# A two-layer graph network on one NeuronCore: the first edge pass takes its scores in one tile of 32 nodes by 512 edges

## The reference, cut to what matters

```python
h  = node_features @ node_fc_W + node_fc_b
hs, hd = h[src], h[dst]
a = jnp.sum(hs * hd, axis=-1)                      # one score per edge
g = sigmoid(... edge features ...)                 # three relation logits per edge
alpha = _seg_softmax(a, dst, n)                    # softmax over the edges of one destination
beta  = _seg_softmax(g, dst, n)
s_att = jnp.einsum('ed,kdf->ef', hs, node_att_W)
h_att = segment_sum(alpha[:, None] * s_att, dst) / kk
t_rel = jnp.einsum('ed,mdf->emf', hs, rel_att_W)
h_rel = segment_sum(jnp.einsum('em,emf->ef', beta, t_rel), dst) / mm
h_red = relu(concatenate([h_att, h_rel]) @ out_fc_W + out_fc_b)
```

## Time and profile before

| | |
|---|---|
| median of the timed runs | 4027.08 us |
| profiled execution | 4024.09 us, span 4022.5 us |
| mean granted clock of TensorE | 0.76 of full |
| PE busy | 2824.3 us, 70% |
| PE weight loads | 1855.1 us, 46% |
| DVE | 1767.3 us, 44% |
| POOL | 1684.4 us, 42% |
| ACT | 1341.8 us, 33% |
| DMA queues | 12.1% and 12.1% of 16 engines |

### The profile page before, as it was taken

The page is one execution under the profiler, slowest core; times in us unless marked ns, Lnnn a source line. Parts: engine busy times, 40 slices in busy tenths (PEclk is TensorE's granted clock), DMA queues, the critical chain, the costliest instruction groups (busy, mean ns, idle before and its releaser), DMA issues. The chain is left out here.

```text
span 4022.5 us, 76683 instructions
## 1 busy us (share of the span) xinstructions
PE 2824.3 (70%) x19840; PEld 1855.1 (46%) x19840; DVE 1767.3 (44%) x5359; ACT 1341.8 (33%) x4047; POOL 1684.4 (42%) x1702
## 2 busy tenths in 40 slices
PE   7899996577666666676777885666666666666664
PEld 4333432344444444444444584454555554455542
DVE  8845501223222322232322445465555656555564
ACT  3677774122222222222222321222222222222222
POOL 0000002544444444444444300466666666666661
PEclk9999998677777877777777855567676667776776
DMA  7111111222222222222222200222222222222221
GB/s 96 43 45 45 53 49 44 72 85 82 81 79 81 82 81 81 81 80 82 82 84 86 89 4 15 68 72 71 72 72 71 71 72 70 70 73 70 72 68 27
DMA packets 315466, 273.42 MB, mean 68 GB/s; under 512 B 195937, under 2 KB 249718, under 8 KB 315377
## 3 DMA queue, kind: packets, MB, share of 16 engines
q0 software_dynamic: 67328, 137.99, 12.1%
q1 hardware_dynamic: 248049, 134.37, 12.1%
HBM read 184.60 MB, written 9.37 MB: 48 GB/s over the span
## 5 line engine op out<-in xcount | busy, mean ns | idle before, releaser
L1007 POOL DMA_INDIRECT y_wide<-h_table,src_g x784 | 749.3, 956 | 1496.0 <-issue 858.5
L1535 POOL DMA_INDIRECT att_acc<-kv_table,rec_sb x880 | 911.6, 1036 | 468.2 <-issue 237.6
L1581 PE MATMUL bank<-att_acc,probT 128*128 128x193 f32 x1760 | 525.8, 464 | 123.9 <-DVE probT L1699 66.6
L1581 PEld LDWEIGHTS bank<-att_acc,probT 128*128 128x128 f32 x1760 | 434.2, 274 | 185.4 <-DVE probT L1699 110.6
L1069 PE MATMUL bank<-hs,hot_w 128*96 128x129 f32 x2368 | 435.4, 334 | 57.1 <-issue 56.7
L1069 PEld LDWEIGHTS bank<-hs,hot_w 128*96 128x96 f32 x2368 | 348.7, 200 | 155.8 <-issue 146.0
L1168 DVE TENSOR_SCALAR_CACHE_REDUCE junk<-bank,m_st 128x128 bf16<-128x128 f32 x296 | 103.0, 348 | 705.8 <-remote 610.1
L680 ACT ACTIVATE att_acc<-bank,bias 128x512 f32<-128x512 f32 x588 | 350.4, 695 | 37.6 <-PE bank L559 33.0
L559 PE MATMUL bank<-rel_acc,wc 64*128 64x512 f32 x1176 | 360.1, 627 | 0.2 <-ACT att_acc L680 0.2
L1039 PE MATMUL bank<-identf,hs 128*128 128x128 f32 x1184 | 244.3, 325 | 155.7 <-issue 120.1
L1116 ACT ACTIVATE prob<-bank,m_new 128x128 f32<-128x128 f32 x296 | 108.8, 368 | 719.6 <-DVE junk L1168 510.3
(11 more groups left out here) (297 smaller groups left out, 4233.8 us busy)
## 6 DMA issues: line engine op xcount, KB each, us to landing
hs<-y_wide SPq DMA_DIRECT2D x296, 258.0 KB
rel_acc<-in_edge_attr SPq DMA_DIRECT2D x97, 256.0 KB, 2.6
att_acc<-kv_table,rec_sb POOLq DMA_INDIRECT x880
y_wide<-h_table,src_g POOLq DMA_INDIRECT x784
qb<-q_table SPq DMA_DIRECT2D x220, 48.0 KB
hbT<-hT_table SPq DMA_DIRECT2D x296, 16.0 KB
rec_sb<-rec SPq DMA_DIRECT2D x220, 4.0 KB
kv_table<-att_acc SPq DMA_DIRECT2D x25, 96.0 KB, 1.6
```

What stands on the lines that cost most here:

```text
L1007: pool.indirect_dma_start(out=landed_rows[:, k * GT + j, 0:D], out_offset=None, in_=h_table, in_offset=bass.IndirectOffsetOnAxis(ap=src_g[ ...
L1535: pool.indirect_dma_start(out=row_v[:, k % RING, j, 0:KV], out_offset=None, in_=kv_table, in_offset=bass.IndirectOffsetOnAxis(ap=rec_v[:, ...
L1581: last = pe.matmul(bank[4 + k % 2][0:BN, 0:KV + 1], probT_v[:, k % 2, j, :], row_v[:, k % RING, j, AD:RK], start=(j == 0), stop=(j == GT - 1))
```

## The change

The first edge pass works on one score tile of 32 nodes by 512 edges a step. So each node has one row, one running maximum and one shrink factor. The maximum is carried from step to step in `m_old` (a ring of four columns) rather than stored per window; where the next step has another window, `reset0` adds 1e33 and so starts it anew. The exponentials are 32 by 512 and are turned back by four transposes into the first 32 columns of `both`; DVE writes the 96 weighted one-hot columns beside them, and one set of four fp32 matmuls with 128 stationary columns makes the attention sum (lanes 0 to 31) and the three relation sums (lanes 32 to 127) at once, into one of four banks. One accumulator `sum_acc` takes both; its shrink factor is 1 in the lanes of the relations. The gather ring has 16 groups and lies in an area of its own name, `area_b`, and is released by PE's `stepped`; the counter `copied` goes. The merging stage needs no joining of maxima and no lane selection: four 128-wide transposes per block.

The core of the diff:

```diff
-RING0 = 8
+RING0 = 16
...
-            hot_w = sb2("hot_w0", [128, HW, GT * M * WN])
-            prob = sb2("prob", [128, 2, 128])
-            probT = sb2("probT", [128, 2, 128])
-            m_new = sb2("m_new", [128, 2])
+            both = sb2("both", [128, 4, GT, (1 + M) * WN])
+            prob = sb2("prob", [WN, 2, GE])
+            m_new = sb2("m_new", [WN, 4])
+            m_old = sb2("m_old", [WN, 4])
...
# POOL
-                            pool.wait_ge(copied, last_step + 1)
+                            pool.wait_ge(stepped, last_step + SU0 + 1)
...
-                        if g == RING0 - 1:
-                            pool.memset(area_b, 0.0).then_inc(cleared_b, 1)
...
# PE
+                    def turn_back(s, k):
+                        n = s * SU0 + k
+                        pe.wait_ge(prob_done, n + 1)
+                        pe.sem_inc(ticks, 1)
+                        for j in range(GT):
+                            last = pe.transpose(bank[3][:, j * WN:(j + 1) * WN], prob[:, k % 2, j * 128:(j + 1) * 128], identf[0:WN, 0:WN])
+                        last.then_inc(probT_ps, 1)
...
+                        tile = bank[1 + k % 2][0:WN, :]
+                        pe.matmul(tile, far[0:1, 0:WN], far[0:1, WN:], start=True, stop=False)
+                        for j in range(GT):
+                            pe.matmul(tile[:, j * 128:(j + 1) * 128], onehot_v[:, k % SH, j, :], big_ident[:, :], start=False, stop=False)
+                        pe.matmul(tile, hbT[:, k % SH, :], hsT[:, k % 2, :], start=False, stop=True).then_inc(score_ps, 1)
...
+                            last = pe.matmul(bank[4 + k % 4][:, 0:D + 1], both[:, k % 4, j, :], hs[:, k % SH, j, :],
+                                             start=(j == 0), stop=(j == GT - 1))
...
                     def body(s, k, edge):
                         if inside(edge, k, 0, SU0):
                             turn_back(s, k)
+                        if inside(edge, k, 2, SU0):
+                            scores(*step_of(s, k, 2, SU0))
                         if inside(edge, k, 3, SU0):
                             turn(*step_of(s, k, 3, SU0))
-                        if inside(edge, k, 2, SU0):
-                            scores(*step_of(s, k, 2, SU0))
                         if inside(edge, k, 0, SU0):
-                            relations(s, k)
-                            attention(s, k)
+                            sums(s, k)
...
# ACT
+                        act.activation(prob[:, k % 2, :], bank[1 + k % 2][0:WN, :], ACT.Exp, scale=-1.0,
+                                       bias=m_new[:, q:q + 1]).then_inc(prob_done, 1)
+                        act.activation(shrink[0:WN, q:q + 1], m_old[:, q:q + 1], ACT.Exp, scale=-1.0, bias=m_new[:, q:q + 1])
+                        act.activation(m_old[:, after:after + 1], m_new[:, q:q + 1], ACT.Identity,
+                                       bias=reset0[:, bass.ds(n + 1, 1)]).then_inc(carried, 1)
...
# DVE
+                        v.wait_ge(carried, n + 1)
+                        v.wait_ge(score_ps, n + 1)
+                        v.tensor_scalar(junk[:, :], bank[1 + k % 2][0:WN, :], m_old[:, q:q + 1], None, ALU.min, ALU.min,
+                                        accum_out=m_new[:, q:q + 1]).then_inc(max_done, 1)
...
+                        one = flat(sum_acc[:, bass.ds(within(b, WINS - 1), 1), :])
+                        v.scalar_tensor_tensor(one, one, shrink[:, q:q + 1], bank[4 + q][:, 0:D + 1],
+                                               ALU.mult, ALU.add).then_inc(summed, 1)
...
# merging: sums of one block
                         for k in range(PER):
-                            pe.matmul(o[:, k * WN:(k + 1) * WN], att_acc[:, b * PER + k, 0:D], lane_sel[:, 0, :], start=True, stop=True)
-                        for k in range(PER):
-                            last = pe.transpose(o[:, BN + k * M * WN:BN + (k + 1) * M * WN], rel_acc[0:M * WN, b * PER + k, 0:D],
-                                                identf[0:M * WN, 0:M * WN])
+                            last = pe.transpose(bank[b % 3][:, k * 128:(k + 1) * 128], sum_acc[:, b * PER + k, 0:D], identf[:, :])
```

More of the change, by code:

```diff
@@ L35 @@
 SH = 8
-HW = 2
-RING0 = 8
+RING0 = 16
 ROUNDS0 = STEPS0 + 8
@@ L1040, in turn, with sums @@
                         last.then_inc(hsT_ps, 1)
-                    def scores(s, k):
+                    def sums(s, k):
                         n = s * SU0 + k
-                        pe.wait_ge(hsT_done, n + 1)
-                        pe.wait_ge(hot_done, n + 1)
-                        pe.wait_ge(prob_done, n + 1)
-                        pe.matmul(bank[1 + k % 2][:, 0:128], far_rows[0:1, 0, :], far_rows[0:1, 1, :], start=True, stop=False)
+                        pe.wait_ge(probT_done, n + 1)
@@ L1049, in scores @@
                         for j in range(GT):
-                            pe.matmul(bank[1 + k % 2][j * WN:(j + 1) * WN, 0:128], onehot_v[:, k % SH, j, :], big_ident[:, :],
-                                      start=False, stop=False)
-                        for j in range(GT):
-                            last = pe.matmul(bank[1 + k % 2][j * WN:(j + 1) * WN, 0:128], hbT[:, k % SH, :], hsT[:, k % 2, j * 128:(j + 1) * 128],
-                                             start=False, stop=True)
@@ L1055, in scores @@
-                        last.then_inc(score_ps, 1)
-                    def turn_back(s, k):
-                        n = s * SU0 + k
-                        pe.wait_ge(prob_done, n + 3)
-                        pe.wait_ge(probT_done, n + 1)
-                        pe.sem_inc(ticks, 1)
-                        pe.transpose(bank[3][:, 0:128], prob[:, k % 2, :], identf[:, :]).then_inc(probT_ps, 1)
-                    def relations(s, k):
-                        n = s * SU0 + k
-                        pe.wait_ge(hotw_done, n + 1)
-                        pe.wait_ge(summed, 2 * n + 6)
-                        for j in range(GT):
-                            pe.matmul(bank[6 + k % 2][0:M * WN, 0:D + 1], hot_w_v[:, k % HW, j, :], hs[:, k % SH, j, :],
-                                      start=(j == 0), stop=(j == GT - 1))
@@ L1072, in attention @@
-                    def attention(s, k):
-                        n = s * SU0 + k
-                        pe.wait_ge(probT_done, n + 2)
-                        for j in range(GT):
-                            last = pe.matmul(bank[4 + k % 2][j * WN:(j + 1) * WN, 0:D + 1], probT[:, k % 2, j * WN:(j + 1) * WN],
-                                             hs[:, k % SH, j, :], start=True, stop=True)
+                            last = pe.matmul(bank[4 + k % 4][:, 0:D + 1], both[:, k % 4, j, :], hs[:, k % SH, j, :],
+                                             start=(j == 0), stop=(j == GT - 1))
@@ L1387, in _ @@
-                    step(v.tensor_scalar(none[:, :], some[:, :], -1.0, 1.0, ALU.mult, ALU.add))
-                    step(v.tensor_tensor(z_att[:, :], bank[2][:, 0:WALL], none[:, :], ALU.add))
-                    step(v.reciprocal(z_att[:, :], z_att[:, :]))
-                    step(v.tensor_tensor(fac[:, :], fac[:, :], z_att[:, :], ALU.mult))
+                    step(v.tensor_scalar(none[:, :], sum_acc[:, :, D], 0.0, None, ALU.is_le))
+                    step(v.tensor_scalar(some[:, :], none[:, :], -1.0, 1.0, ALU.mult, ALU.add))
@@ L1392, in rescale @@
+                    step(v.tensor_tensor(fac[:, :], sum_acc[:, :, D], none[:, :], ALU.add))
+                    step(v.reciprocal(fac[:, :], fac[:, :]))
                     def rescale(n):
                         wins = slice(n * PB * PER, (n + 1) * PB * PER)
-                        one = att_acc[:, wins, 0:D]
+                        one = sum_acc[:, wins, 0:D]
                         v.tensor_tensor(one, one, fac[:, wins].unsqueeze(2).to_broadcast([128, PB * PER, D]), ALU.mult).then_inc(scaled, 1)
-                        one = rel_acc[0:M * WN, wins, 0:D]
```

218 lines of the change are left out of this document (67 added, 151 removed).

## The result

The changed kernel takes 4043.67 us (median of 5 runs, 4025.13 to 4050.89), the kernel before 4025.25 (5 runs): ratio 1.0044, interval 1.0025 to 1.0064. It is a little slower, where 3910 was forecast. The profiled execution has a span of 4038.1 us, 15.6 over that of before.

What follows compares the result with a forecast made beforehand. Long POOL gather runs that almost stop the other queues were taken to bound the first pass. From 4024 us, 78 less in the pass and 39 less in merging, plus 3 for the median, gave 3910 us; range 3690 to 4085.

Steps and rivals of the forecast that it cites:

- What bounds the kernel: First edge pass: long POOL gather runs almost stop the other queues, so pass time is nearly gather time plus step time.
- PE, per step: First pass: PE's step grows from 2.66 to 3.37 us, bounds 3.0 to 4.0, with the score at 0.85.
- Instructions per step: First pass: instructions per step fall from 79 to 56, against an allowance of about 115 per 10 us gather run.
- The cycle: First pass, two gather groups and three steps: 16.15 us instead of 17.05, with 2.05 steps fitting in the run.
- the lag until PE resumes and the low clock after the stop: First pass, POOL's pause after a gather run: 2.95 us beyond the steps' own time, taken as unchanged.
- The merge: Merging the sums: start 8 us shorter, 25 blocks 31 us less at 2.76 us each; 39 us less in all.
- The deeper ring: First pass, gather ring of 16 groups instead of 8: priced at nothing beyond the start, since POOL is held by PE.
- A: Rival, first pass: the stop comes by time, 3 us into the run; cycle 18.1 us, total 4085 us; chance 0.18.
- B: Rival, first pass: the stop mostly goes away as gather runs break up; total 3625 us; chance 0.20.
- C: Sizes off one way: a step of 4.0 us gives 3980, of 3.0 gives 3870; within the forecast's 0.58.
- D: Rival, each step: ACT's Identity forces table reloads beside Exp; some hundreds of us higher; chance 1 in 50.

Runs made afterwards that it cites:

- 1: The changed kernel with only the first 16 groups gathered, later groups reusing what lies in the ring: 3379.66 us.
- 2: The kernel before with only the first 8 groups gathered, later groups reusing what lies in the ring: 3321.83 us.
- 8: The changed kernel with the turn ahead of the scores and twelve one-element DVE memsets added per step: 3954.25 us, ratio 0.9819 (0.9596 without the memsets).
- 16: The kernel before with a short pause (memset of 8 elements and a wait) after each group of four gathers: 3840.9 us, ratio 0.944.
- 12: The changed kernel with each 128-column merge transpose made as four 32-column matmuls, on the chip where the kernel before takes 3191.28 us: 3277.93 us.
- experiment 9: The changed kernel with a ring of 8 groups instead of 16, on the chip where the kernel before takes 3191.28 us: 3100.52 us, ratio 0.9708.

## Why the prediction was wrong

*What bounds the kernel* was right: gathers that stop the other queues, some 700 us of it (1, 2).

*PE, per step* was right: 3.35 against 3.37, in part by luck, since terms that were off by up to 0.11 us cancel. The trace decides between the two scores: 0.96 us, three times the 0.32 of the four tiles and nearer to the row's 0.85. By the Trainium skill (TensorEngine Tiling (Array Packing), Theoretical Speedup), up to fourfold, the estimate was 1.28.

*Instructions per step*, and that their count matters, are borne out: twelve more hurt by the amount that the count asks for (8), and the kernel with 56 bears short runs better than the one with 79 (16). Neither run rules out every other reason.

*The cycle* failed, in the step that took over "the lag until PE resumes and the low clock after the stop", 2.95 us, and put 2.05 steps in a run. Both silently assumed that PE issues as freely as before. The diff also put the scores ahead of the turn; I listed that line in the change and priced it at nothing, without a reason and without asking who waits for the turn's copy and what covers it. The copy had nearly a whole step of cover and has 1.36 us now. In the run PE stands for ACT when the stop catches the copy, the clock falls, and a step of 5.1 us follows. Measured: 99 to 103 instructions in the two runs shown, 95 in the mean (115), so 1.8 steps in a run; a pause of 8.4 to 8.8 us (6.15), and with it a lag of 8.6 - 1.2 x 3.35 = 4.6 us (2.95). With the order undone, the pass came out 64 us shorter (78 forecast) and the total at 3875 (3910).

*The merge* had its mechanism right and its clock wrong: I doubled the rows of the full clock because the earlier trace rows stood at the low one. The low clock belonged to the work that the change removed: what is left runs at 1.00 from the third block on, and narrow instructions put back keep it at 0.50 (12). Until PE starts, the merge came 7.5 us shorter (8 forecast), in the blocks 62 (31): together 70, not 39. The Trainium skill (TensorE: Matmul & The Clock Gate, Part 1) has the clock set by how busy PE has been. The trace of experiment 12 does not agree in that form: PE is busy 196 of 196 us, at 0.50.

*The deeper ring* at nothing: nearly, up to 30 us on the wrong side.

*The rivals.* A gave the right cycle (18.1, measured 18.4) by a wrong mechanism: in the cycles shown the stop came 3.0 us into the run before and 7.4 us into it now, so time does not set it. The prediction held for A that the stop is "so regular at 3 us in every cycle"; I had read that off too few cycles. In the 62 runs of eight of the kernel before between 1000 and 2200 us, the first 0.7 us in which PE, ACT and DVE start nothing begins 2.8 to 6.5 us into the run, but after 79 to 110 instructions, in half of the runs 95 to 100. The first 1.5 us of that kind in the changed kernel begins at 4.4 to 9.5 us in 57 of 59 runs, in half of them after 91 to 99 instructions (shorter standstills are common there, so I took the longer measure). The count is steadier than the time. A's 4085 is closer than my 3910 by luck and would have taught the wrong thing. The chance I gave to a slower kernel, 0.19, rested mostly on it. B was half right: with the turn first the runs of eight fall from 77 in the kernel before to 63, and where pauses break up the rest the total is 3602. That this is near B's 3625 is partly luck, since POOL's pauses cost time that B did not have. C's and D's conditions did not come; ACT shows no gap between Identity and Exp (1513.28 and 1513.47 in its timeline follow on each other).

Open: what on the chip stops the queues, and why one chip did not do it; whether that one never does is not known either. The changed kernel with its own ring and merge was not run there; experiment 12 took 220.4 us from its last sums to the end of its last folded product and experiment 9 took 42.4, so with its merge put back it would be about 3100, an estimate, 91 us under before and the same as with the ring of 8.

## What to carry to other kernels

When a diff reorders two steps of an engine, write down what each one waits for on the other engines and how much work covers that wait, before and after: a copy that a whole step of work hides while nothing is held is exposed as soon as its engine is held up. Before pricing a stretch at a low clock, ask which of its instructions keep it there, and whether the change removes just those. Long runs of indirect gathers can cost more by what they do to other queues than by themselves; a pause of 1.6 us after each group of four took this kernel to 0.895 of before on one chip, and on another, where nothing is held, the kernel before from 3191 to 3437 us.

## What the hardware showed that I had not expected

- Two chips differed by a fifth on the same program: 4025 us and 3191 us for the kernel before. On the second, 784 gathers ran in a row, one in 1.27 us, and no queue was held; on the first, PE, ACT and DVE start almost nothing for 4.3 us of a run of eight (4 matmuls).
- A memset of 0.2 us and the wait for it, 1.6 us without a gather, is enough to keep the queues of the changed kernel going: 3875 to 3602 us, more than a longer pause (3782).
- PE without a gap for 196 us at a granted clock of 0.50, with 32-column fp32 matmuls making up most of its work.
